# Layer 1 of a two-layer graph network on one core: gathered tiles packed full, 196 a chunk instead of 220, and products addressed by a register

## The reference, cut to what matters

```
h = relu(layernorm(x))
x = x + segment_sum((h @ W0)[src] * edge_weight, dst) + b0
h = relu(layernorm(x))
xt = einsum('ni,rio->rno', h, W1)               # 8 relations
x = x + relu(segment_sum(xt[edge_type, dst], src) + b1)
```

## Time and profile before

| | |
|---|---|
| Median of three runs | 1430.05 us |
| The profiled execution | 1437.78 us, span 1435.9 us, mean granted clock 0.873 |
| PE / DVE / POOL / ACT busy | 1093.0 / 1012.6 / 961.0 / 791.9 us |
| POOL: DMA_INDIRECT rows | 880 instructions, 856.6 us |
| Chain that ended last | POOL 26%, PE 25%, DVE 16%, issue 15%, ACT 10% |

### The profile page before, as it was taken

One profiled execution on the slowest core, in us unless ns is written; L12 is line 12 of the kernel. 1 busy time (PEld: TensorE's weight loads), 2 busy tenths in 40 slices (PEclk: granted clock), 3 DMA queues, 4 the chain that ended last, 5 costly groups with the idle time before them and its releaser, 6 DMA issues.

```text
span 1435.9 us, 25703 instructions
## 1 busy us (share of the span) xinstructions
PE 1093.0 (76%) x5255; PEld 761.2 (53%) x5255; DVE 1012.6 (71%) x3454; ACT 791.9 (55%) x2226; POOL 961.0 (67%) x967
## 2 busy tenths in 40 slices
PE   3578867777778758889899996776767678778875
PEld 3467746555567646767677773444444333333332
DVE  8899588888888896867776757666666454445453
ACT  4899757777878356777777536666666000000000
POOL 0687567766767776566566507777777777777773
PEclk9799979999999989999999998999899675666565
DMA  4011143333333534555565753333333733333336
GB/s 133 2 28 32 40 151 103 94 87 88 95 90 98 98 90 136 158 156 168 162 181 155 147 158 98 105 106 104 106 104 105 90 119 106 103 106 106 104 113 133
DMA packets 85462, 156.30 MB, mean 109 GB/s; under 512 B 18726, under 2 KB 57220, under 8 KB 85380
## 3 DMA queue, kind: packets, MB, share of 16 engines
q0 software_dynamic: 44640, 115.56, 31.7%
q1 hardware_dynamic: 40740, 39.77, 8.3%
HBM read 122.19 MB, written 32.99 MB: 108 GB/s over the span
## 4 chain that ended last, share of the span: by engine, by line
POOL 26%; PE 25%; DVE 16%; issue 15%; ACT 10%; DMA 4%; DVEq 2%; POOLq 1%; ACTq 0%; SPq 0%
POOL rows L375 26%; PE bank L1069 10%; ACT oh_f L415 8%; PE bank L1193 7%; PE bank L1060 6%; DVE x_sb L753 3%; DVE oh_m L738 3%; DVE oh_t L703 2%; DVE oh_p L693 2%; DMA rows<-table,idx_ring 2%; DMA x_sb<-in_x_dram 1%; DVE scan L586 1%; DVEq L745 1%; DVE oh_f L698 1%; PE bank L1041 1%
## 5 line engine op out<-in xcount | busy, mean ns | idle before, releaser
L375 POOL DMA_INDIRECT rows<-table,idx_ring x880 | 856.6, 973 | 391.3 <-issue 252.4
L1069 PE MATMUL bank<-rows,oh_m 128*128 128x256 f32 x1760 | 669.4, 476 | 270.4 <-DVE x_sb L753 120.7
L1069 PEld LDWEIGHTS bank<-rows,oh_m 128*128 128x128 f32 x1760 | 329.6, 223 | 482.6 <-DVE oh_m L741 171.1
L753 DVE TENSOR_TENSOR x_sb<-x_sb,bank 128x256 f32 x880 | 362.8, 412 | 9.1 <-PE bank L1069 8.1
L1060 PE MATMUL bank<-oh_t,oh_f 125*128 125x220 bf16 x2425 | 344.8, 268 | 16.4 <-ACT oh_f L415 12.4
L415 ACT ACTIVATE oh_f<-oh_p,ew_part 125x128 bf16<-125x128 f16 x850 | 324.2, 686 | 44.4 <-DVE oh_p L693 41.5
L1060 PEld LDWEIGHTS bank<-oh_t,oh_f 125*128 125x128 f16 (+1 forms) x2425 | 262.4, 120 | 106.4 <-ACT oh_f L415 20.3
L415 ACT ACTIVATE oh_f<-oh_p,hi 125x128 f16<-125x128 f16 x400 | 269.8, 674 | 43.4 <-DVE oh_p L693 41.5
L448 ACT ACTIVATE idx_ring<-idx 128x4 int32 (+1 forms) x220 | 50.5, 233 | 436.9 <-PE bank L1069 421.4
L703 DVE TENSOR_SCALAR oh_t<-iota_t,pos_t 125x220 bf16<-125x220 f16 x725 | 216.8, 306 | 79.7 <-PE bank L1069 78.7
L415 ACT ACTIVATE oh_f<-oh_p,lo 125x128 f16<-125x128 f16 x400 | 271.1, 678 | 0.0
(11 more groups left out here) (157 smaller groups left out, 619.9 us busy)
## 6 DMA issues: line engine op xcount, KB each, us to landing
table<-stage SPq DMA_DIRECT2D x100, 256.0 KB, 2.8
rows<-table,idx_ring POOLq DMA_INDIRECT x880, 2.8
table<-stage SPq DMA_DIRECT2D x25, 128.0 KB
x_sb<-in_x_dram SPq DMA_DIRECT2D x1, 3072.0 KB
out_dram<-x_sb SPq DMA_DIRECT2D x4, 640.0 KB
w_sb<-in_L_gnn_weight_dram SPq DMA_DIRECT2D x2, 1024.0 KB, 6.6
scattered<-pay,place POOLq DMA_INDIRECT x75
out_dram<-x_sb SPq DMA_DIRECT2D x1, 512.0 KB
```

What stands on the lines that cost most here:

```text
L375: pool.indirect_dma_start(out=rows[:, u, :], out_offset=None, in_=tables[s // CH][:, :], in_offset=bass.IndirectOffsetOnAxis(ap=idx_ring[: ...
L753: V.tensor_tensor(acc[:, ds(off, D)], acc[:, ds(off, D)], message_bank(u), ALU.add).then_inc(s_acc, 1)
L1069: TE.matmul(message_bank(u), oh_m[:, u % OR, :], rows[:, u, :], start=True, stop=True).then_inc(s_msg, 1)
```

## The change

**Layout of chunks 2 and 3.** Edges are packed without gaps between blocks into TG = 196 tiles. A tile may then hold edges of two blocks, so products and sums go by 220 *steps*: a step is one (tile, block) pair. Blocks are taken in ascending order of their edge count, the 53-node block last; the block of rank k begins at edge `begin`, its steps are `begin // 128 + k` to `end // 128 + k`. One-hots, banks and adds stay one a step. A step whose tile is shared reads the same gathered tile as its neighbour.

**POOL** gathers 196 tiles a chunk in straight code, with its index column taken from `idx` itself, into a ring of RR = 32 slots (`rows1`, over the memory of `w1_hi` and `w1_lo`). Every fourth gather waits for a step that is surely past the slot's last use (24 steps on), and each chunk for `s_index`. ACT's refills (L448) fall away in phases 2 and 3.

**PE** reads four slot offsets into registers for each four steps, and takes the moving operand of the product at the register's offset. A step waits for a new tile only where one may be new (`NEED`). Its loops over groups are unrolled in phases 2 and 3, as are DVE's in phase 3.

**Indices by step become indices by tile**: 2 PE transposes, 2 copies, 2 PE products with a one-hot `at_tile`, one copy. **Ranking** of chunks 2 and 3 has other, longer chains. **Outputs** go block by block in rank order, each behind its last step, into a buffer of its own and out with a 128 KB store; 25 stores in place of 6.

```diff
@@ constants
+    TG = -(-EP * CC // P)
+    RR = 32
+    BEGIN = [EP * CC * k // (NB - 1) for k in range(NB)]
+    NEED = [t - min(k for k in range(NB) if k == NB - 1 or t - k <= BEGIN[k + 1] // P) for t in range(T)]
+    ENDED = [BEGIN[k + 1] // P + k + 1 for k in range(NB - 1)] + [T]
...
@@ sync
-            for g in range(NB // TU):
-                sp.wait_ge(s_final, min((g + 1) * TU, NFULL))
...
+            for k in range(NB - 1):
...
+                sp.wait_ge(s_final, k + 1)
+                sp.dma_start(out[ds(row, P), :], done_block(k)).then_inc(s_out, 16)
@@ gpsimd
+            for s in range(CH, NS):
+                pool.wait_ge(s_index, s + 1)
+                for t in range(TG):
+                    g = (s - CH) * TG + t
+                    if t % RF == 0:
+                        if g + RF > RR:
+                            m, before_t = divmod(g + RF - 1 - RR, TG)
+                            pool.wait_ge(s_msg, (CH + m) * T + min(T - 1, before_t + NB - 1) + 1)
+                        pool.nop(nofuse=True)
+                    pool.indirect_dma_start(
+                        out=rows1[:, g % RR, :], out_offset=None, in_=table1[:, :],
+                        in_offset=bass.IndirectOffsetOnAxis(ap=idx[s % 2][:, t:t + 1], axis=0),
+                    ).then_inc(s_rows[g % RR], 16)
@@ vector, ranking of chunks 2 and 3
                 if u == 6:
-                    block_offsets(s)
-                if u == 8:
-                    tile_counts(s)
-                if u == 13:
-                    ended_blocks(s)
+                    order_keys(s)
+                if u == 12:
+                    begin_blocks(s)
                 if u == 18:
-                    tile_offsets(s)
+                    step_tiles(s)
...
+            def order_keys(s):
...
+                dve.wait_ge(s_total, s + 1)
+                V.scalar_tensor_tensor(key_row[:, :], RANK[0:NB, 0:NB], 32.0, order_row[:, :], ALU.mult, ALU.add)
+                V.tensor_copy(col_f[:, :], column(0))
+                V.tensor_scalar(col_plus[:, :], column(0), float(RANK_UNIT), None, ALU.add)
+                step(V.scalar_tensor_tensor(key_col[:, :], column(0), 32.0, order_col[:, :], ALU.mult, ALU.add))
+                step(V.tensor_scalar(fewer[:, :], key_row[:, :], key_col[:, 0:1], None, ALU.is_gt))
+                V.tensor_scalar(tiles_before[:, :], fewer[:, :], col_plus[:, 0:1], None, ALU.mult).then_inc(s_fewer, 1)
...
@@ vector, positions(s), for s >= CH: 8 operations in place of 4
+                    step(V.tensor_scalar(tile_i, tmp_i[:, :], 7, 255, ALU.logical_shift_right, ALU.bitwise_and))
+                    step(V.tensor_copy(key_hi[:, :], tile_i))
+                    step(V.tensor_scalar(rank_i, tmp_i[:, :], RANK_UNIT.bit_length() - 1, None, ALU.logical_shift_right))
+                    step(V.tensor_copy(row_f[:, :], rank_i))
+                    V.tensor_tensor(pos_t[s % 2][:, :], key_hi[:, :], row_f[:, :], ALU.add)
...
@@ vector, last group of phases 1 and 2
+            def turn_index(s):
+                dve.wait_ge(s_idxturned, s - CH + 1)
+                for h in range(2):
+                    last = V.tensor_copy(idx_T[0:steps_of(h), h, :], index_steps(h))
+                last.then_inc(s_idxT, 1)
+
+            def tile_index(s):
+                dve.wait_ge(s_idxtile, s - CH + 1)
+                V.tensor_copy(idx[s % 2][:, 0:TG], index_tiles).then_inc(s_index, 1)
...
+                        if u == 3:
+                            decode_index(m + 1)
+                        if u == 7:
+                            turn_index(m + 1)
+                        if u == 9:
+                            decode_local(m + 1)
+                        if u == 11:
+                            tile_index(m + 1)
@@ vector, output(t)
+                k = ENDED.index(t)
+                dve.wait_ge(s_acc, (NS - 1) * T + t + 1)
...
+                V.scalar_tensor_tensor(done_block(k), got, 0.0, own, ALU.max, ALU.add).then_inc(s_final, 1)
@@ tensor
+            def turn_index(s):
+                pe.wait_ge(s_idxstep, s - CH + 1)
+                steps = idx[s % 2][:, :].bitcast(f32)
+                for h in range(2):
+                    last = TE.transpose(index_steps(h), steps[:, h * P:h * P + steps_of(h)], ident[:, :])
+                last.then_inc(s_idxturned, 1)
...
+            def slots(s, t):
+                _, got = nc.values_load_multi_w_load_instructions(
+                    slot_off[s - CH][0:1, t:t + LAG], engines=[mybir.EngineType.PE], min_val=0,
...
+            def step_message(m, t, slot):
+                u = t % U
+                pe.wait_ge(s_ohm, t + 1 + m * T)
+                if t == 0 or NEED[t] > NEED[t - 1]:
+                    g = (m - CH) * TG + NEED[t]
+                    pe.wait_ge(s_rows[g % RR], 16 * (g // RR + 1))
+                if u % 2 == 0:
+                    pe.wait_ge(s_acc, t + 3 - RING + m * T)
+                TE.matmul(message_bank(u), oh_m[:, u % OR, :], rows1_flat[:, ds(slot, D)],
+                          start=True, stop=True).then_inc(s_msg, 1)
...
@@ tensor, chain(s, u): begin_blocks (3 products) at u = 9, step_tiles (5 products) at u = 15
+            def turns(s, u):
+                if u == 4:
+                    turn_index(s)
+                if u == 8:
+                    tile_index(s)
```

More of the change, by code:

```diff
@@ L977, in _ @@
             phase(2)
+            agg_flat = agg1[:, :, :].rearrange("p b d -> p (b d)")
             def output(t):
-                for b in range(NB):
-                    if DONE[b] == t:
-                        if t == T:
-                            dve.wait_ge(s_acc, NS * T + 1)
-                        V.scalar_tensor_tensor(x1_sb[:, b, :], agg1[:, b, :], 0.0, x1_sb[:, b, :],
-                                               ALU.max, ALU.add).then_inc(s_final, 1)
-            def early_outputs():
-                for t in range(DONE[0], (TI - 1) * U - LAG + 1):
-                    output(t)
-            phase(3, early_outputs, output)
-            last_sums(3, output)
+                if t not in ENDED:
+                    return
+                k = ENDED.index(t)
+                dve.wait_ge(s_acc, (NS - 1) * T + t + 1)
+                if k < NB - 1:
+                    _, (off,) = nc.values_load_multi_w_load_instructions(
+                        done_off[0:1, k:k + 1], engines=[mybir.EngineType.DVE], min_val=0, max_val=(NB - 1) * D,
+                        skip_runtime_bounds_check_because="done_off holds block numbers times D")
+                    got, own = agg_flat[:, ds(off, D)], x1_flat[:, ds(off, D)]
+                else:
+                    got, own = agg1[:, k, :], x1_sb[:, k, :]
+                V.scalar_tensor_tensor(done_block(k), got, 0.0, own, ALU.max, ALU.add).then_inc(s_final, 1)
+            for i in range(TI):
+                message_group(NS - 1, i, first=i == 0, last=i == TI - 1, summed=output)
+            last_sums(NS - 1, output)
         @block.tensor
@@ L1075, in group @@
                 for u in range(U):
-                    message(m, i, u, first)
+                    if m < CH:
+                        message(m, i, u, first)
+                    else:
+                        if u % LAG == 0:
+                            got = slots(m, i * U + u)
+                        step_message(m, i * U + u, got[u % LAG])
                     if sort and u >= PELAG:
@@ L1210, in side @@
                         late_sums(CH + 1, u)
+                        turns(CH, u)
                 if i == SI - 2:
@@ L1219, in _ @@
                 table_part(t)
-            phase(2)
-            phase(3)
+            for m in range(CH, NS):
+                pe.wait_ge(s_decoded, m + 1)
+                sort = m + 1 < NS
+                if sort:
+                    pe.wait_ge(s_index, m + 1)
+                    sort_edges(m + 1, "open")
+                for i in range(SI):
+                    group(m, i, sort=sort)
+                if sort:
+                    sort_edges(m + 1, "close")
+                group(m, SI, side=(lambda i, u: turns(m + 1, u)) if sort else None)
 _INS = ['x', 'src', 'dst', 'edge_type_8', 'edge_weight', 'L0_gnn_weight', 'L0_gnn_bias', 'L1_gnn_weight', 'L1_gnn_bias']
```

171 lines of the change are left out of this document (139 added, 32 removed).

## The result

The changed kernel takes a median of 1374.84 us (1372.84 to 1381.43, 4 runs) against 1427.87 (1422.03 to 1442.0, 4 runs) before. The ratio is 0.962, 95% interval 0.954 to 0.970: 53 us less, where 62 were forecast. A later measurement on one chip gave 1375.13 against 1426.83, ratio 0.963 (0.958 to 0.968). The profiled execution took 1381.43 us with a span of 1379.6, 56.3 less than the profiled one of before.

What follows compares the result with a forecast made beforehand. POOL's back-to-back gathers, 1.257 us each, were taken to bound phases 2 and 3, work beside them phases 0 and 1. Terms -60.3 - 8.3 - 2.7 + 7 + 2 = -62.3 us took 1430.05 to 1368 us, range 1353 to 1390.

Steps and rivals of the forecast that it cites:

- D: Phases 0 and 1: longer ranking chains, positions and index turning add +7 us, between 0 and +12.5.
- A: Phases 2 and 3: 48 fewer gathers, each worth 1.257 us of POOL, give -60.3 us.
- B: End of phase 3: the last gather lands in 2.8 us instead of 11.1, -8.3 us.
- C: End of the kernel: smaller last stores leave sooner, -2.7 us, between 0 and -3.5.
- E: Hand-over from chunk 2 to chunk 3: POOL waits for the index with 1.4 us margin; +2 us, 0 to +5.
- F: Phases 2 and 3: the step loop does 220 steps in 196 gathers' time, 1.10 us against 1.12 a step; cost 0.
- The rival in which phase 2 is paced by its steps at 1.24 us: Phase 2: PE at 1.01 us plus an open register load of 0.23 a step; total 1392 us, chance 0.16.
- The rival of a draining PE: Phase 2: register loads wait until PE has drained, 1.46 to 1.60 us a step; total 1443 to 1474, chance 0.05.
- The sign that I had named for F: Phase 2 profile: PE's waits still end with DMA; ending with DVE one-hots or issue, POOL awaiting PE, means step-loop pacing.
- the second case: Phase 2 paced by its step loop at 1.24 us a step, not by POOL; total 1392 us, chance 0.16.

Runs made afterwards that it cites:

- its version: Kernel before, with the index raised to at least the partition's number so an empty tile's 128 places fetch different rows: 1429.67 us, one run.
- late turns: Changed kernel with the turning of chunk 2's index moved from phase 1's last group into the table tail: median 1371.08 us, ratio 0.957.
- split chain: On top of late turns, four ranking operations made at program start and begin_blocks spread over u = 12 to 15: median 1367.65 us, ratio 0.959.

## Why the prediction was right, and where not

**The mechanism and the sign were right.** 1374.84 lies in the range, 6.8 us above the forecast. By terms, in the two profiled executions, in which messages 20 to 100 happen to take the same 120.8 us (that is luck: with the changed kernel's second profile, where they take 109.3, D would read +2.4):

| term | forecast | measured |
|---|---|---|
| A, 48 gathers | -60.3 | -60.1 |
| B, last landing | -8.3 | -7.7 |
| C, last stores | -2.7 | -1.3 |
| D, front | +7 | +12.8 |
| E, hand-over | +2 | 0 |
| sum | -62.3 | -56.3 |

**A** held to 0.2 us, and the experiment with 24 more gathers closes it from the other side.

**B and C** are split at the start of the last messages: landing and wait went from 11.2 us (1415.42 to 1426.64) to 3.5 (1371.65), and the rest from 9.3 to 8.0. I had taken the median landing of 2.8, but 3.5 us pass from the last gather's start to its product. The last tile's 88 places of row 0 are not the reason: with distinct rows it was 3.4 (1415.15 to 1418.54). The last store takes some 4.4 us to the end, not the 3.2 taken from the landing of a table store.

**D is the step that failed: its parts were right, the discount was not.** I priced the items at +12.5 and took +7, since "the groups of the ranking chain leave DVE some air" and PE is "fed by table products too". Next to nothing hid:

| part of D | priced | measured |
|---|---|---|
| chain of chunk 2, messages 100 to 120 | 3.4 + 0.5 | +4.1 |
| `positions` of chunk 2, in messages 120 to 220 | 1.2 | +0.8 |
| chain of chunk 3, messages 320 to 340, both at clock 1.00 | 2.9 + 0.5 | +3.4 |
| turning of the index, from message 420 on | 3.5 to 4 | +5.1 (+4.1 at clock 1.00) |

The chain made twice cost 2.8 to 4.5 us more, and the turning, moved away, costs 0.7. Over messages 220 to 320 and 340 to 420, where nothing is added, the two profiles differ by -2.4 and +1.5, with small differences of the granted clock; that is the noise of this comparison. A busy share of 84% does not mean that 16% are free. In messages 100 to 120 PE's message products wait in the main for DVE's adds: 7.0 us before, 8.0 in the changed kernel, 11.4 with the chain twice. PE waits for DVE's one-hot and add, DVE for PE's product, and what is put into DVE lengthens the round. The place that did hide DVE's share of the turning was the tail, where no message waits for DVE; PE's share shows there too.

**E** cost nothing, since the index was ready sooner than I reckoned. The copy that releases it, and the first gather that needs it:

```profile
1115.84 0.36 DVE L856 CAST idx<-bank 128x196 int32<-128x196 f32 x1 [2.13 <-PE bank L1212]
```

```profile
1122.79 0.95 POOL L435 DMA_INDIRECT rows<-table,idx  x1 [0.30 <-PE bank L1276]
```

It ends at 1116.2, and POOL wants it at 1122.8: a margin of 6.6 us and not 1.4. I had let the 11 steps of the last group run at the gathers' pace of 1.12 us and added 4.9 us for decoding and turning on top. Message 200 started at 1104.7 and message 211 at 1117.5, so the steps with the decoding among them took 12.8 us in all, and the index was ready before message 211. After its wait of 1.7 us for the decoding PE made three messages in 1.9 us: the loop can run faster than the gathers (0.97 with a sort column in each step, 0.73 without), and in that group there are no columns left, so it makes up part of what the decoding takes.

**F** was right in kind: reckoned 1.01 without the register load and 1.10 with it, measured 0.95 and 0.97. The first difference is the clock: with the measured 0.98 in place of 0.91 the same sum, 0.96 x 0.95 + 0.04 x 1.26, gives 0.96. The rival in which phase 2 is paced by its steps at 1.24 us fails on the loads: I let them stand in the open at 0.90 us, and they show 0.10 each. The rival of a draining PE fails with it. The granted clock of the changed kernel was 0.97 in phase 2 and 0.79 in phase 3, against 0.91 and 0.64 before; what that gave was not measured apart. The sign that I had named for F reads less clearly than I had thought: of PE's waits in phase 2, those for a gather's landing fell from 45.2 to 25.8 us and those for DVE's one-hots and adds rose from 16.1 to 29.2, and still the gathers' spacing did not move. And the range was drawn carelessly: 1390 was said to take in nearly all of the second case, whose own figure is 1392.

## What to carry to other kernels

Where one engine issues at a fixed spacing with nothing but "issue" between, an instruction taken away is worth that spacing as long as the other engines keep up, and the test of the cover is to take away half of them and see at what pace the rest runs. Small operations put into a group in which two engines wait for each other showed whole here, whatever the busy shares; put them where nobody waits for the engine that makes them, and count what they add to the engine that is busy there. Compare stretches at the same granted clock where there are several profiles. Judge an edit by the length of the stretch that holds it and not by a point in time: identical code ahead of it can move by more than its price.

## What was not expected of the hardware

The same code took 109.3 or 120.8 us from message 20 to message 100, with a granted clock of 1.00 or 0.90 in that stretch (the pairs of windows above), and other profiles fall to one side or the other: of the ten of the changed kernel and its versions, eight lie at 109.3 to 112.7 us and two at 120.8 and 122.7; the kernel before and its version have 120.8 both. Nearly all of the difference is PE's busy time, 79.7 or 90.6 us for the same instructions. The profiled runs' totals follow it: of the two with 120.8 and 122.7 they are 1381.43 and 1387.24, of the other profiles of the same three kernels (changed, late turns, split chain) 1368.68 to 1373.11. Runs without a profile fall apart in a similar way, those of the kernel before into 1422 to 1430 and 1437 to 1442 us; that this is the same cause is likely and not shown, since no profile of the kernel before lies in the faster group. What decides it is open.

A run of indirect gathers in which all 128 places name one row lands late: the messages of a run came 1.7 us apart and the last of all landed after 11.1 us, against 2.8 for others and 3.25 with distinct rows. The 88 places of the one partly empty tile cost next to nothing: 3.5 us from its gather to its product, against 3.4 with distinct rows.
